# A four-layer graph network: first-layer row stores ahead of the x requests, and h0 tiles two pieces earlier

## The reference

```python
h = jnp.maximum(_layernorm(x, axis=-1), 0.0)
x = x + _L0_gnn_ref(h, adj, L0_gnn_weightr, L0_gnn_weightd, L0_gnn_bias)
...
    A = adj + jnp.eye(N, dtype=adj.dtype)
    deg = A.sum(axis=1)
    dinv = jnp.where(deg > 0, jax.lax.rsqrt(deg), 0.0)
    A = A * dinv[:, None] * dinv[None, :]
    R = x[:SIZE_U] @ weightr
    D = x[SIZE_U:] @ weightd
    h = jnp.concatenate([R, D], axis=0)
    out = A @ h + bias
    return jax.nn.leaky_relu(out, negative_slope=LEAKY_SLOPE)
```

## Time and profile before

| | |
|---|---|
| median of 3 runs | 2111.86 us (2110.57 to 2112.67) |
| the profiled execution | 2112.05 us, of which the span is 2110.3 us |
| PE busy | 2052.6 us, 97% of the span |
| DVE busy | 1326.5 us, 63% |
| ACT busy | 1012.9 us, 48% |
| POOL busy | 53.6 us, 3% |

### The profile page before, as it was taken

One profiled execution on the slowest core, in us unless ns is written; L12 is line 12 of the kernel. 1 busy time (PEld: TensorE's weight loads), 2 busy tenths in 40 slices (PEclk: granted clock), 3 DMA queues, 4 the chain that ended last, 5 costly groups with the idle time before them and its releaser, 6 DMA issues.

```text
span 2110.3 us, 26133 instructions
## 1 busy us (share of the span) xinstructions
PE 2052.6 (97%) x10560; PEld 1493.7 (71%) x10560; DVE 1326.5 (63%) x2040; ACT 1012.9 (48%) x1333; POOL 53.6 (3%) x88
## 2 busy tenths in 40 slices
PE   5999989999999999999999899999999999999998
PEld 4888865555545555554555588888888888888887
DVE  6855440000044242434548899999999999999674
ACT  6755440000020000001104679797888788787873
POOL 0011340000000000000000000000000000000000
PEclk9999999999999999999999999999999999999999
DMA  9997352010311223301157645444445444351200
GB/s 376 381 349 278 111 202 48 21 41 21 100 50 56 65 64 96 117 31 61 48 109 313 170 160 207 138 180 145 180 144 179 165 140 180 132 212 65 100 20 11
DMA packets 102393, 288.25 MB, mean 137 GB/s; under 512 B 45184, under 2 KB 52096, under 8 KB 85760
## 3 DMA queue, kind: packets, MB, share of 16 engines
q1 hardware_dynamic: 96896, 278.19, 38.3%
q10 hardware_dynamic: 5376, 8.39, 1.3%
HBM read 245.11 MB, written 33.06 MB: 132 GB/s over the span
## 4 chain that ended last, share of the span: by engine, by line
PE 90%; DVE 3%; DMA 2%; ACT 2%; POOL 1%; issue 1%; SPq 0%; ACTq 0%; POOLq 0%; DVEq 0%
PE ps L1822 41%; PE ps L1733 32%; PE ps L1593 7%; PE ps L1750 7%; PE ps L1792 2%; DMA h_spill<-work 1%; POOL work L649 1%; PE ps L1699 1%; DMA feat<-in_adj 1%; PE ps L1671 1%; PE ps L1660 1%; ACT big L686 0%; DMA big<-in_adj_t 0%; POOL work L664 0%; DVE feat L1426 0%
## 5 line engine op out<-in xcount | busy, mean ns | idle before, releaser
L1733 PE MATMUL ps<-big,feat 128*128 128x512 fp8e4 x3072 | 671.1, 381 | 11.3 <-DMA feat<-h_spill 7.1
L1733 PEld LDWEIGHTS ps<-big,feat 128*128 128x128 f16 x3072 | 301.4, 98 | 375.0 <-issue 12.9
L1822 PE MATMUL ps<-big,work 128*128 128x257 f32 x2048 | 450.9, 381 | 4.9 <-ACT work L961 4.9
L1822 PE MATMUL ps<-big 128*128 128x257 f32 x2048 | 449.4, 380 | 3.5 <-ACT big L961 3.5
L1822 PEld LDWEIGHTS ps<-big,work 128*128 128x128 f32 x2048 | 388.4, 190 | 60.8 <-issue 4.8
L1822 PEld LDWEIGHTS ps<-big 128*128 128x128 f32 x2048 | 388.3, 190 | 59.6 <-ACT big L961 4.4
L1593 PE MATMUL ps<-feat,big 128*128 128x256 f16 x2048 | 224.7, 273 | 0.0
L1593 PEld LDWEIGHTS ps<-feat,big 128*128 128x128 fp8e4 x2048 | 199.9, 98 | 23.4
L686 ACT ACTIVATE big<-big 128x2048 bf16<-128x2048 f32 (+1 forms) x124 | 182.3, 1487 | 13.2 <-DMA big<-in_adj_t 12.9
L953 ACT ACTIVATE big<-feat,uv_sb 128x512 f32<-128x512 f32 x256 | 163.3, 710 | 22.5 <-PE ps L1822 22.5
L953 ACT ACTIVATE work<-feat,uv_sb 128x512 f32<-128x512 f32 x256 | 163.4, 713 | 16.5 <-PE ps L1822 15.8
(11 more groups left out here) (165 smaller groups left out, 1365.9 us busy)
## 6 DMA issues: line engine op xcount, KB each, us to landing
big<-in_adj_t SPq DMA_DIRECT2D x64, 1024.0 KB, 4.9
feat<-in_adj SPq DMA_DIRECT2D x56, 1024.0 KB, 6.9
big<-in_adj_t SPq DMA_DIRECT2D x80, 512.0 KB, 9.6
h_spill<-work SPq DMA_DIRECT2D x31, 512.0 KB, 3.6
feat<-h_spill SPq DMA_DIRECT2D x31, 512.0 KB, 4.7
work<-in_adj_t SPq DMA_DIRECT2D x27, 512.0 KB, 6.7
x_spill<-work SPq DMA_DIRECT2D x24, 512.0 KB, 2.7
feat<-in_adj_t SPq DMA_DIRECT2D x21, 512.0 KB, 8.6
```

Of the source, the lines that this page charges most:

```text
L1733: ins = mm(ps[:, bank + f, :], parts[:, j, h, f * P:(f + 1) * P], adj_units[:, c, j, :], start=(fresh and h == 0), stop=(end and h == 1), ...
L1822: ins = mm(ps[:, 4 * s + t, 0:YW], quads[k % RING][:, jj, t * P:(t + 1) * P], Yb[:, j, s, :], start=(j == 0), stop=(j == NT - 1), skip_gro ...
```

## The change

On SP, in the loop over the chunks of layer 0, the store of rows c - 1 now stands ahead of the refill of x. Two constants of the opening are altered: every h0 tile, its copy and the copy of y0 move two pieces ahead (`FIRST_TILE` 2 to 0), and the statistics move one piece back (`STATS_AHEAD` 4 to 3). The small product of the attention weights (`rows_of_a`) and its copy move with them.

```diff
-    FIRST_TILE = 2
-    STATS_AHEAD = 4
+    FIRST_TILE = 0
+    STATS_AHEAD = 3
...
                     for c in range(NC - 1):
                         store_x(c)
+                        if c > 0:
+                            store_h(c - 1)
                         if c + 3 < NC:
                             refill(c, c % 2, c // 2)
-                        if c > 0:
-                            store_h(c - 1)
                     load_weights(1)
                     store_h(NC - 2)
...
-                if n == 17:
+                if n == 14:
                     act.wait_ge(wa_ps_ready, 1)
...
-                if q == 6:
+                if q == 5:
                     rows_of_a()
```

## The result

The changed kernel takes 2118.74 us (median of 7 runs, 2117.72 to 2119.8) against 2111.86 us before: ratio 1.0033, 95% interval 1.0022 to 1.0044. It is slower by 6.9 us. The forecast was 2113.4, which is 1.5 us slower, with a range of 2105.5 to 2118.5. The profiled execution took 2118.82 us, its span is 2117.0 us.

The account below looks back on a forecast made before the run. PE was taken to bound the kernel, with DVE the full engine in the opening. From 2112.05 us, -9.6 for the stores and +11.0 for the opening gave 2113.4 us, range 2105.5 to 2118.5.

Parts of the forecast that it names:

- The new wait for the sums of chunk 4: Late in layer 0, the scaling would want these sums at 258.4, but they come at 259.4; cost 0.8 us.
- the reload was hidden: Ahead of layer 1, the first reloaded features would land at 295.7, 2.1 us before PE finishes layer 0's block products.
- (c, chunk 5): Opening, chunks 5 and 6: the first tile waits for the means, so DVE waits 1.3 and 0.9 us, +2.2.
- (d): Opening, from q = 12: PE is late with products 12 and 13, so DVE's copies wait, +1.7 and +2.5 us.
- (b): Opening, piece 17: DVE's copy 6 waits for a product behind PE's degree sum, +3.8 us, 2.0 at full clock.
- (a): Opening, to piece 16: DVE saves no work and copy 5 finds its product late, about +1.0 us, 0 to 1.5.
- I count 1.0: Opening, q = 10: slow matmuls behind a pause of 4 to 5 us lose 1.9 us, of which 1.0 was counted.
- a pause ahead of q = 12 takes something back: Opening: PE pauses again before q = 12 and so recovers part of the 1.9 us lost at q = 10.
- the third rival: The opening costs more than 13.8 us through half-clock matmuls behind PE's new pauses, and the kernel is slower; chance 0.22.
- 10.0 + 3.8: Opening: PE's forecast delay of 10.0 us plus two unabsorbed slow stretches of 1.9 us each.
- That the opening costs nothing: Rival: the opening costs little or nothing, 0 to 5.4 us, giving 2102.4 to 2107.8 us; chance 0.18.
- That the stores do not help: Rival: another wait holds the rows at 251.64, so the stores give 0 and the time is 2123; chance 0.04.

Follow-up runs that it names:

- e9: The changed kernel with 70 products that nobody reads put into PE's queue ahead of q = 4, 6, 7, 10, 12 and 15; 2111.14 us.
- e2: The changed kernel with the old store order, so the opening's part alone; 2127.23 us, ratio 1.0066.
- e1: The kernel before with only the store order changed, each row store ahead of the x request; 2102.60 us, ratio 0.9957.
- e4: The changed kernel with DVE's copies of y0 back at their old pieces; 2104.12 us, ratio 0.9961.
- e5: The changed kernel with STATS_AHEAD 6, so the means again stand three pieces ahead of the tiles; 2106.95 us, ratio 0.9977.
- e8: The kernel before with the new store order and STATS_AHEAD 3, tiles and copies in their old places; 2102.56 us, ratio 0.9961.
- e10: The kernel before with the new store order and only DVE's copies of y0 two pieces early; 2114.34 us, ratio 1.0016.

## Why the prediction was wrong

**The stores: right in mechanism and size.** -9.6 us was forecast and -9.5 us measured by themselves, as a pause of PE (7.0) and its slow clock behind it (2.6). The new wait for the sums of chunk 4 is there too (0.48 us on ACT, where 0.8 had been counted), and the reload was hidden.

**The opening's queues: right in place, a little small in size, and their sum right by luck.** The single waits were forecast as 1.3 (c, chunk 5), 0.9 (chunk 6), 1.7 and 2.5 (d), and measured without slow matmuls as 1.05, 1.40, 1.58 and 2.21. For (b) I had said 2.0 at full clock; it was 2.08. Only (a) was outside its bounds of 0 to 1.5: DVE closes the counts of chunk 0 (L1133) at 44.68 in e9 instead of 42.39, 2.3 us late. The waits gave PE a delay of 10.0 us, and with the clock kept up the second degree sum came 10.2 us late. But the 10.0 held 1.8 us of a slow product in (b). Without it the forecast for the queues was 8.2, beside 10.2 by the profiled executions and 8.8 by the medians.

**The step that failed: the clock, "I count 1.0".** I took one slow stretch of 1.9 us, behind the pause of over 4 us at q = 10, and let half of it be absorbed, because most of the other pauses were to be shorter than those that the rows showed. With the 1.8 in (b) the forecast held 2.8 us of slow matmuls; the runs showed 6.5 (7.7 by the medians). The price of one stretch was right, 1.5 to 2.4 us measured. Their number was wrong: the clock fell behind the pauses at q = 4, 6, 7, 10 and 12, one of them 1.51 us long, which made 9.0 us of longer matmuls. It was also wrong that a pause ahead of q = 12 takes something back: PE's product is what DVE's copy waits for, DVE's statistics are what ACT's tile waits for, and the tile is what PE waits for, so a slow product delays its own successors. The waits of DVE grew with it: at piece 11 from none to 0.82, at 15 from 1.02 to 2.65, at 17 from 2.08 to 3.54, at 23 from 1.05 to 3.41, at 27 from 1.40 to 2.99. This was the third rival, to which I had given 0.22, with 10.0 + 3.8 as its threshold, and its sign, PEclk below 1 several times in 25 to 85 us, is there. With both terms as measured the sum is 2112.05 - 9.6 + 10.2 + 6.5 = 2119.2, beside 2118.82 of the profiled execution. That is bookkeeping and no second proof, since 10.2 + 6.5 is the shift of the degree sum in the same traces.

**A path that the prediction left out.** It said that whatever delays or advances the start of the block products moves the end of layer 0 by as much. For a delay this held here. For an advance it does not: in e9 6.5 us at the second degree sum were 4.8 us at layer 1, since PE then waited for the counts of the last adjacency pieces.

The rule of the Trainium skill that I had set beside this ("TensorE: Matmul & The Clock Gate", Part 1), that the slow clock is the default and activity releases it, pointed the right way, and e9 shows it from the other side: added activity kept the clock up and was worth 7.7 us.

**The rivals.** That the opening costs nothing was refuted by e2. That the stores do not help was refuted by e1. Which of the opening's edits does the harm was not among my rivals. In the changed kernel it takes two: with the copies back the rest costs 1.5 us (e4), with the means ahead 4.6 (e5), and with neither cure 16.4. The later means alone cost nothing that shows (e8). Copies moved without their tiles cost 12.8 us even so (e10).

## What to carry to other kernels

In a loop written out for several engines that each work in the order written, a step put earlier than its input is ready is a wait for everything behind it, and on an engine as full as DVE was here the time does not come back: move a consumer forward only with its producer, and the producer only as far as its own inputs allow. When several engines wait for one another in a ring, price each new pause of TensorE twice, once as time and once for slow matmuls that may follow it (1.5 to 2.4 us here where they did), and check whether those matmuls are on the ring. On the engine that issues the DMAs put the store whose data are ready ahead of the request that waits; that is found by asking when a transfer could have been issued, not how long it took.

## What the runs showed of the hardware that had not been expected

Whether the clock falls did not go by the length of the pause. In the changed kernel it fell behind a pause of 1.51 us at 38.85, with 3.52 us for eight matmuls, and stayed up behind one of 2.44 us at 88.69, with 1.14 us for eight transposes. In the run with the stores alone it did not fall behind 2.86 us, at the same place of the program where it had fallen behind 1.32 us before. PE's timeline of that run:

```profile
44.25 0.25 PE L1651 MATMUL ps<-ones,work 128*128 128x1 bf16 x4 [2.86 <-DVE work L1135]
44.36 1.14 PE L1660 MATMUL ps<-ident,work 128*128 128x128 f32 x8
45.34 1.89 PE L1671 MATMUL ps<-work 128*128 128x256 f32 x8
```

The matmuls behind the degree sum cost 1.7 us more before than in this run ((1.75 + 2.99) - (1.14 + 1.89)), though the opening's programs are the same in both kernels. So the number of slow stretches in one profiled execution is a sample, and the 6.5 us above are the difference of two such samples. What decides it was not tried.
